# TensorE announces finished products by a Drain instead of by the last matmul

## What is computed

```
x = x + conv(ln_over_channels(x))         # conv: x * (channel gate + real 2-D Fourier gate)
t = tokens(x)                             # 16384 tokens of 64 channels
t = t + moe(ln(t))                        # 8 experts, top 1, capacity 2560 tokens each
# moe: idx = argmax(softmax(h @ gate_w + gate_b)); pos = place in the expert's buffer
#      hmid = relu(buf @ w1 + b1)         # 64 -> 256
#      ybuf = hmid @ w2 + b2              # 256 -> 64
#      y = ybuf[idx, pos] * prob * (pos < capacity)
x = images(t)
```

## The kernel before

| semaphore | products | who waits for it |
|---|---|---|
| `freq_mm`, `col_mm`, `z_mm` | lines 1002, 1008, 1017 | ScalarE lines 531, 534, 540 |
| `sf_mm`, `cf_mm` | lines 1014, 1029 | VectorE lines 797, 805 |
| `logits_mm` | line 1022 | VectorE line 758 |
| `x_centred`, `x_turned` | lines 973, 981 | ScalarE line 510, VectorE line 814 |
| `base_mm` | line 997 | VectorE line 825 |
| `x1_turned`, `x1_centred` (each twice a turn) | lines 1048, 1054 | ScalarE lines 556, 567 |

## Time and profile before

### The profile page before, as it was taken

How to read it: one execution, slowest core, us unless ns; L and a number is a source line. 1 busy time by engine, 2 the same in 40 slices (tenths; PEclk the granted TensorE clock), 3 DMA queues, 4 the chain that set the end, 5 groups by cost and what they waited for, 6 DMA issues and landing times.

```text
span 488.8 us, 5544 instructions
## 1 busy us (share of the span) xinstructions
PE 278.9 (57%) x1574; PEld 197.2 (40%) x1574; DVE 248.2 (51%) x694; ACT 160.7 (33%) x301; POOL 227.0 (46%) x234
## 2 busy tenths in 40 slices
PE   7695645857191753614004888927477370839562
PEld 5584544846181653504001444514243130415251
DVE  4588366494554836645100367924445161527943
ACT  2362504342150513203000666714254051435300
POOL 0004727317366372757677335374726657461300
PEclk9666656576566665656555999986979586767967
DMA  7991010203000000000003513302113130100089
GB/s 242 413 380 49 29 51 26 60 7 97 11 11 13 4 15 5 15 12 12 13 14 79 105 28 69 82 24 66 44 29 72 40 68 24 34 19 4 7 312 375
DMA packets 38056, 36.16 MB, mean 74 GB/s; under 512 B 27995, under 2 KB 30620, under 8 KB 38034
## 3 DMA queue, kind: packets, MB, share of 16 engines
q1 hardware_dynamic: 29474, 25.71, 17.3%
q0 software_dynamic: 7264, 5.87, 4.2%
q10 hardware_dynamic: 1296, 4.33, 2.2%
HBM read 16.23 MB, written 21.36 MB: 77 GB/s over the span
## 4 chain that ended last, share of the span: by engine, by line
PE 31%; another core or an unknown queue 22%; DVE 18%; issue 12%; ACT 7%; POOL 4%; DMA 3%; SPq 1%; POOLq 0%; ACTq 0%; DVEq 0%
PE psD L1128 8%; PE psX L1115 4%; POOL slot_rows L445 4%; PE psC L1115 4%; PE psT L1048 3%; PE psD L1054 3%; PE psD L1138 3%; DMA x_flat<-token_out 2%; ACT hid L609 2%; DVE x L814 2%; DVE squares L692 2%; DVE rows L754 2%; PE psM L1099 2%; PE psC L973 2%
## 5 line engine op out<-in xcount | busy, mean ns | idle before, releaser
L445 POOL DMA_INDIRECT slot_rows<-rows,slots x128 | 127.2, 994 | 134.4 <-DVE slots L837 96.4
L481 POOL DMA_INDIRECT token_out<-ys,meta x94 | 94.5, 1005 | 96.1 <-DVE ys L913 69.1
L893 DVE TENSOR_TENSOR with_b<-psD,b_all 128x256 f32<-128x256 f32 x40 | 16.9, 423 | 88.9 <-remote 68.7
L1048 PE MATMUL psT<-kc,x 128*128 128x128 f32 x64 | 17.9, 435 | 63.4 <-DVE x L814 57.8
L1138 PE MATMUL psD<-kc,yT 128*128 128x128 f32 x80 | 19.2, 326 | 60.5 <-ACT yT L621 57.4
L1128 PE MATMUL psD<-hid,w_in 128*64 128x256 f32 x320 | 48.8, 431 | 2.1 <-ACT hid L609 2.1
L1138 PEld LDWEIGHTS psD<-kc,yT 128*128 128x128 f32 x80 | 8.6, 150 | 76.4 <-ACT yT L621 64.4
L1048 PEld LDWEIGHTS psT<-kc,x 128*128 128x128 f32 x64 | 11.5, 217 | 68.0 <-DVE x L814 59.2
L609 ACT ACTIVATE hid<-psC,b_in 128x512 f32<-128x512 f32 x40 | 25.5, 692 | 25.3 <-remote 11.0
L609 ACT ACTIVATE hid<-psX,b_in 128x512 f32<-128x512 f32 x40 | 25.4, 690 | 19.9 <-PE psX L1115 7.3
L621 ACT COPY yT<-psD 128x256 f32<-128x256 f32 x40 | 15.0, 374 | 49.9 <-remote 38.0
(11 more groups left out here) (155 smaller groups left out, 534.4 us busy)
## 6 DMA issues: line engine op xcount, KB each, us to landing
slot_rows<-empty_row SPq DMA_DIRECT2D x8, 660.0 KB, 8.1
slot_in<-slot_rows SPq DMA_DIRECT2D x7, 660.0 KB
x_in<-in_x_dram SPq DMA_DIRECT2D x8, 512.0 KB, 3.8
token_out<-zero_row SPq DMA_DIRECT2D x8, 512.0 KB, 10.9
slot_rows<-rows,slots POOLq DMA_INDIRECT x128
w_in<-in_L_ffn_w_dram SPq DMA_DIRECT2D x24, 64.0 KB
token_out<-ys,meta POOLq DMA_INDIRECT x94
x_in<-token_out SPq DMA_DIRECT2D x2, 512.0 KB, 4.0
```

The source lines that it names most:

```text
L445: pool.indirect_dma_start(out=slot_rows, out_offset=bass.IndirectOffsetOnAxis(ap=slots[G.u][:, s:s + 1], axis=0), in_=rows[G.u][:, s, :], ...
L481: pool.indirect_dma_start(out=token_out, out_offset=bass.IndirectOffsetOnAxis(ap=ids[:, UT * b + i, 1:2], axis=0), in_=ys[b][:, i, :], in_ ...
L893: nc.vector.tensor_tensor(with_b2[:], psD[:, 512 * w + 2 * P:512 * w + 2 * P + UT * C].rearrange("p (i c) -> p i c", c=C), b2_all[:, bass. ...
L1048: last = nc.tensor.transpose(psT[:, a * P:(a + 1) * P], x1[:, 2 * t:2 * t + 2, :].rearrange("p s c -> p (s c)"), ident)
```

## The change

Behind each group of products in the first phase (but for the four of the setup) and in all expert units stands a Drain on TensorE, and the group's semaphore update is on the Drain and no longer on the last matmul. A Drain is an instruction of the engine's sequencer that ends when the engine has finished what was issued before it. Nothing else changes: the products, their order, the waits ahead of them and every other engine's program are the same. The setup's four products and the output phase's transposes keep their update on the matmul.

A full turn of the first phase gets 13 Drains, the phase 104 in all (8 for each of nine semaphores, 16 for the two that come twice). A unit gets 4, the second phase 160. That is 264 Drains.

```diff
             def centre_ahead(G, half):
...
                 for t in range(half * TT // 2, (half + 1) * TT // 2):
-                    last = nc.tensor.matmul(psC[:, t * P:(t + 1) * P], pixels(G)[:, t, :], centre,
-                                            start=True, stop=True)
+                    nc.tensor.matmul(psC[:, t * P:(t + 1) * P], pixels(G)[:, t, :], centre,
+                                     start=True, stop=True)
                 if half == 1:
-                    last.then_inc(x_centred, 1)
+                    nc.tensor.drain().then_inc(x_centred, 1)
...
-                last.then_inc(x_turned, 1)
+                nc.tensor.drain().then_inc(x_turned, 1)
...
-                    nc.tensor.matmul(p_sum, ones_b[:], counts[:, E:], start=False, stop=True).then_inc(base_mm, 1)
+                    nc.tensor.matmul(p_sum, ones_b[:], counts[:, E:], start=False, stop=True)
+                    nc.tensor.drain().then_inc(base_mm, 1)
...
-                    last.then_inc(logits_mm, 1)
+                    nc.tensor.drain().then_inc(logits_mm, 1)
...
-                last.then_inc(slots_turned, 1)
+                nc.tensor.drain().then_inc(slots_turned, 1)
...
-                last.then_inc(hid_mm, 1)
+                nc.tensor.drain().then_inc(hid_mm, 1)
...
-                last.then_inc(y_mm, 1)
+                nc.tensor.drain().then_inc(y_mm, 1)
...
-                last.then_inc(y_turned, 1)
+                nc.tensor.drain().then_inc(y_turned, 1)
```

More of the change, by code:

```diff
@@ L1002, in a_turn @@
                     nc.tensor.matmul(p_freq, mean_q[:].rearrange("p q s -> p (q s)"), dft_rows,
-                                     start=True, stop=True).then_inc(freq_mm, 1)
+                                     start=True, stop=True)
+                    nc.tensor.drain().then_inc(freq_mm, 1)
                     pe.wait_ge(xn_done, i + 1)
@@ L1007, in a_turn @@
                     for h in range(2):
-                        last = nc.tensor.matmul(p_col[:, h:h + 1], xn[0:1, h, :], ones[0:1, 0:1], start=True, stop=True)
-                    last.then_inc(col_mm, 1)
+                        nc.tensor.matmul(p_col[:, h:h + 1], xn[0:1, h, :], ones[0:1, 0:1], start=True, stop=True)
+                    nc.tensor.drain().then_inc(col_mm, 1)
                     pe.wait_ge(freq_done, i + 1)
@@ L1013, in a_turn @@
                     for a in range(2):
-                        last = nc.tensor.matmul(p_sf, row_freq[:, a * P:(a + 1) * P], dft_cols[:, a, :],
+                        nc.tensor.matmul(p_sf, row_freq[:, a * P:(a + 1) * P], dft_cols[:, a, :],
                                                 start=(a == 0), stop=(a == 1))
-                    last.then_inc(sf_mm, 1)
-                    nc.tensor.matmul(p_z, cwT[:], col[:], start=True, stop=True).then_inc(z_mm, 1)
+                    nc.tensor.drain().then_inc(sf_mm, 1)
+                    nc.tensor.matmul(p_z, cwT[:], col[:], start=True, stop=True)
+                    nc.tensor.drain().then_inc(z_mm, 1)
                 if T.back:
@@ L1021, in a_turn @@
                     for t in range(TT):
-                        last = nc.tensor.matmul(p_log[:, t * 2 * E:(t + 1) * 2 * E], x1T[:, t * P:(t + 1) * P], cgw[:],
+                        nc.tensor.matmul(p_log[:, t * 2 * E:(t + 1) * 2 * E], x1T[:, t * P:(t + 1) * P], cgw[:],
                                                 start=True, stop=True)
-                    last.then_inc(logits_mm, 1)
+                    nc.tensor.drain().then_inc(logits_mm, 1)
                 if T.front:
@@ L1028, in a_turn @@
                     for h in range(2):
-                        last = nc.tensor.matmul(p_cf[:, h * C:(h + 1) * C], colb[:, h, :], ident[0:C, 0:C],
+                        nc.tensor.matmul(p_cf[:, h * C:(h + 1) * C], colb[:, h, :], ident[0:C, 0:C],
                                                 start=True, stop=True)
-                    last.then_inc(cf_mm, 1)
+                    nc.tensor.drain().then_inc(cf_mm, 1)
                 if T.ahead:
@@ L1114, in up @@
                         at = 512 * a + 2 * P * half
-                        last = nc.tensor.matmul((psX, psC)[w][:, at:at + 2 * P],
+                        nc.tensor.matmul((psX, psC)[w][:, at:at + 2 * P],
                                                 w1_in[u][rows_a, half * P:(half + 1) * P],
                                                 xT[w][rows_a, :], start=True, stop=True)
-                last.then_inc(hid_mm, 1)
+                nc.tensor.drain().then_inc(hid_mm, 1)
             def down(k, local):
@@ L1127, in down @@
                     for a in range(2):
-                        last = nc.tensor.matmul(psD[a * C:(a + 1) * C, 512 * w:512 * w + 2 * P], w2_in[u][:, half, :],
+                        nc.tensor.matmul(psD[a * C:(a + 1) * C, 512 * w:512 * w + 2 * P], w2_in[u][:, half, :],
                                                 hid[w][:, half, a, :], start=(half == 0), stop=(half == 1))
-                last.then_inc(y_mm, 1)
+                nc.tensor.drain().then_inc(y_mm, 1)
             def back(k, local):
```

14 lines of the change are left out of this document (7 added, 7 removed).

## The result

The changed kernel took 543.05 us (median of four runs, 534.39 to 548.25), the kernel before beside it 495.79 us (492.55 to 500.39): a ratio of **1.085**, 95% interval 1.070 to 1.101. The medians are 47 us apart, the wrong way: 417 us was forecast.

What follows compares the result with a forecast made beforehand. It took TensorE's semaphore updates, held while GpSimd issues indirect transfers, to bound the kernel. 491.18 us less 51 (first phase) and 28 (second) gave 412, plus 5.0 for the median 417 us; range 392 to 520, likeliest case to 462.

Steps and rivals of the forecast that it cites:

- the likeliest case: Both phases: with the update off the matmul, all waits for held TensorE signals go; 417 us (392 to 462), chance 0.56.
- the 51 and 28 us: Forecast savings: 51 us in the first phase from shorter turns, 28 us in the second from shorter expert units.
- The Drain itself ends late: Rival, chance 0.14: the product's completion is late, so the Drain and TensorE's groups behind it wait; near 570 us.
- The Drain's price: On TensorE, lost overlap between neighbouring groups plus a restart: 0.3 us per Drain, bounds 0.1 to 0.55.
- The upper bound of 0.55: Most a Drain could cost, in us: a half-clock pass of 0.690 less its slot of 0.2, plus 0.06.
- The rest of the sum: Forecast total over both phases: 491.18 - 51 - 28 = 412 us, plus 5.0 for the median, 417 us.
- 160 and 5 for the first and last: Second phase: 40 units at 4.0 us make 160, with 5 us for the first units and last scatter.
- the upper bound of 24: First phase: us per turn if half of the held time stays, 34 us saved; the value taken was 21.5.
- the 412 forecast for the profiled execution: Whole kernel: the profiled execution's 491.18 us less the savings of 51 and 28.
- The clock: Second phase, sign of a wrong sum: granted clock well below 0.84; eight passes take 1.98 us at the lower clock, against 1.08.

## Why the prediction was wrong

**The step that failed** is the first of the two that the likeliest case rested on: "If the hold lies on the matmul's way to the semaphore, and the sequencer's way is another, all these waits go." The hold isn't on a way. A held product isn't complete for TensorE, and its Drain ends only when it is: update and Drain's end fall together (119.47 and 119.53, 133.88 and 133.95). So no wait went, and none of the 51 and 28 us were saved.

**The rival that came true** is "The Drain itself ends late", given 0.14 and priced at 570 us. It was 543. The mechanism was right, the size 27 us too large. Its first phase was put at 18 us besides the Drains' own cost, and measured 9 to 12 with it; its units at 45 us besides, and measured 24 to 27 with it. Its argument against itself failed: that TensorE goes on for 6.6 us behind a product with a held signal says nothing of that product's completion. In the earlier trace rows the products behind a held one run on, and with a Drain between them they don't (10.67 us of idle time in the profile after).

**The Drain's price** was right: 0.3 us was taken, and 0.27 measured (4 x 0.27 of a unit's 3.89 us). The upper bound of 0.55 wasn't needed.

**The rest of the sum**, had the holds gone, can be read on the chips without them. There the changed kernel takes 435 us, not 417. The units fit: 165 us for all 40, where 160 and 5 for the first and last were forecast. The first phase doesn't: from batch to batch it takes 23.6 us in the mean, near the upper bound of 24 and not at the value, 21.5. The steady turns aren't to blame: the last five steps take (212.35 - 104.16) / 5 = 21.6 us each. The first two take 73.52 - 46.92 = 26.6 and 104.16 - 73.52 = 30.6 us, 14 us more than two at 21.5, and in the kernel before on that chip they take 22.3 and 27.6. So one steady turn was taken for all seven, though the first two were 7 us longer without any Drain, and the Drains added another 7 there. And the first batch was left at 41.82 us, but starts at 46.92. The two make 19 of the 24 us between the 412 forecast for the profiled execution and its 436.40.

One reading was off as well. The last batch of the kernel before begins with the transfer at 241.10; the 243.79 of the earlier trace rows is its second:

```profile
241.10 0.97 POOL L445 DMA_INDIRECT slot_rows<-rows,slots  x1 [0.30 <-issue]
```

So a batch came every (241.10 - 41.82) / 7 = 28.5 us and not every 28.9.

**The clock** stood among the things that could go wrong and had neither a price nor a chance. In the changed kernel's units it fell from 0.84 to 0.71, with Drains in the units alone to 0.81, and on the chip without holds it didn't fall (0.92 before, 0.95 changed). In the kernel with two Drains it alone makes 2.3 us of a unit's 6.45.

**What hangs on the chip.** The hold itself, 22% of the chain in the earlier trace rows, isn't a property of the kernel alone. The kernel before takes 486 to 502 us on some chips and 404 to 408 on others (three and four of the seven on which the experiments ran), and no chip showed both. But each chip ran in one session only, so whether it is the chip or something about the session isn't told apart here. The difference goes with the held completions. What the forecast hoped to save by the change, 79 us, another chip saves with the same kernel (90 us). The Drains lose on both: 8.5% and 7.1%.

## What to carry to other kernels

When a reader waits long after the producer's last instruction has ended, ask first whether the work is complete, and not only past the end that the trace models for it. A Drain waits for completion: it can't make a late signal earlier, and it stops what had gone on behind it (10.67 us of idle time here). Put a group's update on its last matmul; a Drain behind each group costs the overlap with the next group (0.27 us here), and the clock can be lower with it (0.84 to 0.71 here, 0.92 to 0.95 on another chip). And repeat before and after on more than one chip before reading a wait as the kernel's own (496 and 406 us here).

## What the runs showed of the hardware

- On some chips TensorE's products complete up to 11 us after their modelled end while GpSimd issues indirect transfers and for some 3 us behind the last one; later products run in the meantime. On others they don't, with the same program: 496 and 406 us. As many transfers of the same size, issued by SyncE, hold nothing on a chip of the first kind (416.39 us), and few transfers by GpSimd don't either (330.33 us). Whether it is the reading of slot numbers, the order of the places written or the issuing by GpSimd wasn't found.
- The Trainium skill says, on the page PSUM — Partial Sum Buffer (Engine vs sequencer instructions), that engine updates fire on completion and that a Drain waits for the engine to go idle. This case's traces agree: update and Drain let go at 119.47 and 119.53 us, and at 133.88 and 133.95. The completion itself came 10.7 us after the product's modelled end in the changed kernel (118.43 and 129.08 us).
- One program can run a whole stretch at either level of TensorE's clock: with two Drains behind each group it took 411 or 499 us on the same chip, and where it took 499 the granted clock of the units was 0.52.
